# A two-layer gated cross-attention model on one core: in the first expert stage, dispatch three chunks ahead, slot matmuls behind gate and up, other evictions first

## What is computed

```
x = layernorm(x); se = layernorm(slot_embeds) * scale
logits   = einsum('bnd,esd->bnes', x, se)
dispatch = softmax(logits, over the tokens n)
combine  = softmax(logits, over all 1024 slots)
slots    = einsum('bnd,bnes->besd', x, dispatch)
gate     = gelu(slots @ Wg + bg);  up = slots @ Wu + bu
eout     = (gate * up) @ Wd + bd
out      = einsum('bns,bso->bno', combine, eout)
```

## Time and profile before

| | |
|---|---|
| median of 3 runs | 1813.88 us (1812.2 to 1814.11) |
| profiled execution | 1814.76 us |
| its span, first to last instruction | 1813.0 us |
| busy: PE, DVE, ACT, POOL | 1614.1, 1107.4, 951.6, 391.3 us |
| the stage at issue | from 239 to 1141 us of the span |
| gelu, line 883 | 256 times, 687 ns each, with 64 table loads of 1283 ns |

### The profile page before, as it was taken

The page is one execution under the profiler, slowest core; times in us unless marked ns, Lnnn a source line. Parts: engine busy times, 40 slices in busy tenths (PEclk is TensorE's granted clock), DMA queues, the critical chain, the costliest instruction groups (busy, mean ns, idle before and its releaser), DMA issues. The chain is left out here.

```text
span 1813.0 us, 36041 instructions
## 1 busy us (share of the span) xinstructions
PE 1614.1 (89%) x12837; PEld 1316.1 (73%) x12837; DVE 1107.4 (61%) x2407; ACT 951.6 (52%) x1407; POOL 391.3 (22%) x346
## 2 busy tenths in 40 slices
PE   1677589999999999999999999589998878999998
PEld 1566468777777777777777788567777757888887
DVE  6688466656655566655665565446666666555555
ACT  1678356566565666655665666156655644222222
POOL 2234232322222222222222222123222310000000
PEclk9899699999999999999999999799999999999999
DMA  8100000000000000000000000300000020000000
GB/s 221 30 0 1 15 1 2 1 1 2 2 2 3 1 1 2 1 3 1 2 1 2 1 1 2 95 1 1 1 0 0 0 71 1 7 12 6 6 6 12
DMA packets 31171, 23.47 MB, mean 13 GB/s; under 512 B 3161, under 2 KB 28721, under 8 KB 30898
## 3 DMA queue, kind: packets, MB, share of 16 engines
q1 hardware_dynamic: 31026, 21.56, 4.3%
HBM read 19.46 MB, written 2.10 MB: 12 GB/s over the span
## 5 line engine op out<-in xcount | busy, mean ns | idle before, releaser
L762 DVE SCALAR_TENSOR_TENSOR hidden<-psU,b_cols,gelu 128x512 f32<-128x512 f32 x256 | 187.2, 748 | 154.2 <-ACT gelu L883 106.1
L986 PE MATMUL psDown<-w_down,hidden 128*64 128x128 f32 x4096 | 251.9, 276 | 0.8 <-DVE expert_out L768 0.8
L986 PEld LDWEIGHTS psDown<-w_down,hidden 128*64 128x64 f32 x4096 | 220.9, 137 | 18.2 <-issue 8.4
L883 ACT ACTIVATE gelu<-psG,b_cols 128x512 f32<-128x512 f32 x256 | 170.6, 687 | 115.2 <-PE psG L137 112.1
L1635 ACT ACTIVATE silu<-psG 128x512 f32<-128x512 f32 x128 | 76.4, 597 | 213.0 <-PE psG L137 208.1
L717 POOL TENSOR_TENSOR combine_sum<-combine_sum,combineT 128x512 f32<-128x512 f32 x48 | 61.3, 1278 | 493.0 <-ACT combineT L897 493.0
L768 DVE TENSOR_TENSOR expert_out<-psDown,b_down 128x512 f32<-128x512 f32 x128 | 87.9, 687 | 97.6 <-PE psDown L986 93.7
L135 PE MATMUL psG<-slots_hi,w_gate_hi 128*128 128x512 f32 x256 | 110.7, 433 | 26.2 <-DVE slots_lo L863 13.4
L883 ACT ACT_TABLE_LOAD x64 | 82.1, 1283 | 90.1 <-PE psG L137 89.4
L1697 PEld LDWEIGHTS psY<-w_downT,hidden 128*128 128x128 f32 x1024 | 123.9, 191 | 5.8
L1697 PE MATMUL psY<-w_downT,hidden 128*128 128x128 f32 x1024 | 124.3, 275 | 0.0
(11 more groups left out here) (324 smaller groups left out, 3611.6 us busy)
## 6 DMA issues: line engine op xcount, KB each, us to landing
ctx<-in_ctx SPq DMA_DIRECT2D x8, 512.0 KB, 7.1
x<-in_x SPq DMA_DIRECT2D x4, 512.0 KB, 5.6
w_gate_raw<-in_L_ffn_Wg SPq DMA_DIRECT2D x1, 2048.0 KB, 11.9
w_up_raw<-in_L_ffn_Wu SPq DMA_DIRECT2D x1, 2048.0 KB, 17.5
out<-x SPq DMA_DIRECT2D x8, 256.0 KB, 2.3
w_kv<-in_L_xattn_Wkv SPq DMA_DIRECT2D x1, 1024.0 KB
w_down_raw<-in_L_ffn_w_down SPq DMA_DIRECT2D x1, 1024.0 KB, 10.8
kv<-in_L_ffn_slot_embeds SPq DMA_DIRECT2D x1, 512.0 KB, 4.3
```

Source lines behind the costliest of these rows:

```text
L762: dve.scalar_tensor_tensor(hid[e][:, half, :], U[half][:], bcol[:, 1, 4 * ch + 2 * e + half:][:, 0:1], gel[half][:], ALU.add, ALU.mult).th ...
L883: act.activation(gel[half][:], G[half][:], ACT.Gelu, bias=bcol[:, 0, 4 * ch + 2 * e + half:][:, 0:1]).then_inc(s["gelu"], 1)
L986: last = pe.matmul(DN[e * SEQ:(e + 1) * SEQ, j, :], hid[e][:, half, b * SEQ:(b + 1) * SEQ], wd[:, 2 * ch + e, half, :], start=(half == 0 a ...
```

## The change

- Score products, their copies and their maxima all stand at the start of a chunk (`AHEAD`; `FIRST` in the prologue), and alternate between the banks of `psM`.
- Dispatch is made three chunks ahead instead of two. Its transposes are made two chunks ahead, go into `psU1` behind down of half 0, and its copy stands behind `slots_hi` on ScalarE. TensorE waits for that copy ahead of the second gate product.
- The slot matmuls stand directly behind gate and up; down of half 0, combine and transposes follow them.
- `expert_out` of half 0 stands ahead of `mtok`, of `finish` and of `slots_lo`; `slots_lo` stands ahead of the sum of dispatch. `slots_hi` and `slots_lo` signal each half.
- `mb` stands behind down of half 1. x is turned through `psG1`.
- At the end of a chunk ScalarE computes a gelu of one column into `warm`, which nobody reads.

```diff
-EARLY = ((), (), (), (), (2,), (), (5,), (7,))
-LATE = ((), (), (0,), (1,), (3,), (4,), (6,), ())
+AHEAD = ((), (), (), (0, 1), (2, 3), (4,), (5, 6), (7,))
+FIRST = ((), (), (), (0,), (1,), (2,), (3, 4), (5, 6, 7))
...
-    ones = sb("ones_col", [P, 1])
+    ones, warm = sb("ones_col", [P, 1]), sb("warm_col", [P, 1])
...
     G0 = G[0][:].rearrange("p (t s) -> p t s", t=OP)
+    G1 = G[1][:].rearrange("p (t s) -> p t s", t=OP)
+    U1 = U[1][:].rearrange("p (t s) -> p t s", t=OP)
...
-        return M0 if has_core(o) else (M0, M[:, 1, :], G[0][:], G[1][:])[n % 4]
+        if has_core(o):
+            return M[:, 1 if n in (1, 3, 6) else 0, :]
+        return (M[:, 0, :], M[:, 1, :], G[0][:], G[1][:])[n % 4]
...
-                if exists(o, ch, 2):
-                    need(pool, s["eb_inv"], k + 3)
-                    e = eb[ch % 2]
+                if exists(o, ch, 3):
+                    need(pool, s["eb_inv"], k + 4)
+                    e = eb[(ch + 1) % 2]
                     pool.tensor_tensor(e[:], e[:], over(rb[:], SEQ, 2), ALU.mult).then_inc(s["eb_normed"], 1)
...
                 if has_head(o):
-                    for n in EARLY[ch]:
+                    for n in ahead(o, ch):
                         column_max(o, n)
                 if has_core(o):
...
-                if has_head(o):
-                    for n in LATE[ch]:
-                        column_max(o, n)
-                    if ch == 1:
-                        need(dve, s["lnT_hi"], o + 2)
-                        need(dve, s["lb"], 8 * (o + 1))
-                        dve.tensor_tensor(lnT[1][:], G[0][:], lnT[0][:].bitcast(F32), ALU.subtract
-                                          ).then_inc(s["lnT_lo"], 1)
-                    if ch == CH - 1:
-                        need(dve, s["top_t"], o + 2)
-                        need(dve, s["mb"], o + 1)
-                        dve.tensor_reduce(mtok[:], G0, AX.X, ALU.max).then_inc(s["mtok"], 1)
+                if has_core(o):
+                    expert_out(k, 0, ch)
+                if ch == CH - 1 and has_head(o):
+                    need(dve, s["top_t"], o + 2)
+                    need(dve, s["mb"], o + 1)
+                    dve.tensor_reduce(mtok[:], G0, AX.X, ALU.max).then_inc(s["mtok"], 1)
                 if done:
                     finish(o - 1)
-                if has_core(o):
-                    expert_out(k, 0, ch)
+                if exists(o, ch, 1):
+                    i = (ch + 1) % 2
+                    need(dve, s["up"], 4 * k)
+                    for b in range(2):
+                        need(dve, s["sl_hi"], 2 * (k + 1) + b + 1)
+                        hi, lo = (sl[i][n][:].rearrange("p e (t b) n -> p e t b n", b=2)[:, :, :, b, :] for n in (0, 1))
+                        dve.tensor_tensor(lo, M[:, b, :].rearrange("p (t e n) -> p e t n", t=OP, e=2),
+                                          hi.bitcast(F32), ALU.subtract).then_inc(s["sl_lo"], 1)
+                if ch == 1 and has_head(o):
+                    need(dve, s["lnT_hi"], o + 2)
+                    need(dve, s["lb"], 8 * (o + 1))
+                    dve.tensor_tensor(lnT[1][:], G[1][:], lnT[0][:].bitcast(F32), ALU.subtract
+                                      ).then_inc(s["lnT_lo"], 1)
...
-                if exists(o, ch, 1):
-                    i = (ch + 1) % 2
-                    need(dve, s["sl_hi"], k + 2)
-                    need(dve, s["up"], 4 * k)
-                    for b in range(2):
-                        hi, lo = (sl[i][n][:].rearrange("p e (t b) n -> p e t b n", b=2)[:, :, :, b, :] for n in (0, 1))
-                        last = dve.tensor_tensor(
-                            lo, M[:, b, :].rearrange("p (t e n) -> p e t n", t=OP, e=2), hi.bitcast(F32), ALU.subtract)
-                    last.then_inc(s["sl_lo"], 1)
                 if done:
                     keep_fresh(c, dve, o - 1, fresh, bn, s["x_new"], s["bn"])
...
         act.activation(work[:, 0, :], work[:, 0, :], ACT.Sqrt).then_inc(s["inv_b"], 1)
+        act.wait_ge(s["ones_ready"], 1)
...
-                    for n in EARLY[ch]:
+                    for n in ahead(o, ch):
                         keep_raw(o, n)
                 if has_core(o):
                     for e in range(2):
                         for half in range(2):
                             gelu(k, e, ch, half)
-                if has_head(o):
...
-                        keep_raw(o, n)
-                if exists(o, ch, 1):
-                    need(act, s["td"], k + 2)
-                    need(act, s["sl"], k + 1)
-                    act.copy(dn[:], M1).then_inc(s["d_ready"], 1)
...
-                if exists(o, ch, 2):
-                    need(act, s["shifted"], k + 3)
-                    act.activation(eb[ch % 2][:], eb[ch % 2][:], ACT.Exp).then_inc(s["eb_exp"], 1)
+                if exists(o, ch, 3):
+                    need(act, s["shifted"], k + 4)
+                    act.activation(eb[(ch + 1) % 2][:], eb[(ch + 1) % 2][:], ACT.Exp).then_inc(s["eb_exp"], 1)
                 if has_core(o):
...
                 if exists(o, ch, 1):
                     need(act, s["sl"], k + 2)
                     need(act, s["up"], 4 * k)
-                    need(act, s["sl_lo"], k)
+                    need(act, s["sl_lo"], 2 * k)
                     for b in range(2):
                         hi = sl[i][0][:].rearrange("p e (t b) n -> p e t b n", b=2)[:, :, :, b, :]
-                        last = act.copy(hi, M[:, b, :].rearrange("p (t e n) -> p e t n", t=OP, e=2))
-                    last.then_inc(s["sl_hi"], 1)
+                        act.copy(hi, M[:, b, :].rearrange("p (t e n) -> p e t n", t=OP, e=2)).then_inc(s["sl_hi"], 1)
+                if exists(o, ch, 2):
+                    need(act, s["td"], k + 3)
+                    need(act, s["sl"], k + 2)
+                    act.copy(dn[:], U1).then_inc(s["d_ready"], 1)
+                if ch == 1 and has_head(o):
+                    need(act, s["tx"], o + 2)
+                    need(act, s["lb"], 8 * (o + 1))
+                    act.copy(lnT[0][:], G[1][:]).then_inc(s["lnT_hi"], 1)
                 if ch == CH - 1 and has_head(o):
                     need(act, s["mb"], o + 2)
                     need(act, s["ct_sub"], 8 * (o + 1))
                     act.copy(mb[:], G[1][:]).then_inc(s["mb_ready"], 1)
+                if has_core(o) and exists(o, ch, 1):
+                    act.activation(warm[:], ones[:], ACT.Gelu)
         walk(act, body)
...
-            back = 1 if has_core(o) else 4
+            back = (2 if n in (1, 3, 6) else 1) if has_core(o) else 4
             need(pe, s["raw"], j + 1 - back)
...
-            need(pe, s["sl_hi"], k + 1)
-            need(pe, s["sl_lo"], k + 1)
+            need(pe, s["sl_lo"], 2 * (k + 1))
...
-                    for n in EARLY[ch]:
-                        need(pe, s["sl_hi"], k + 1)
-                        need(pe, s["sl_lo"], k + 1)
+                    for n in ahead(o, ch):
+                        need(pe, s["sl_lo"], 2 * (k + 1))
                         scores(o, n)
                 if has_core(o):
                     if ch == 0:
                         need(pe, s["mtok"], o + 1)
                         need(pe, s["mb_ready"], o + 1)
                         need(pe, s["den_inv"], o)
-                    if ch == 2 and has_head(o):
-                        need(pe, s["lnT_hi"], o + 2)
-                        need(pe, s["lnT_lo"], o + 2)
                     for e in range(2):
                         for half in range(2):
+                            if e == 0 and half == 1 and exists(o, ch, 1):
+                                need(pe, s["d_ready"], k + 2)
+                            if e == 0 and half == 1 and ch == 2 and has_head(o):
+                                need(pe, s["lnT_lo"], o + 2)
                             gate_up(k, e, ch, half)
-                if has_head(o):
-                    for n in LATE[ch]:
-                        scores(o, n)
-                if has_core(o) and exists(o, ch, -1):
-                    combine(k - 1, 1, (ch - 1) % CH)
                 if exists(o, ch, 1):
-                    need(pe, s["eb_normed"], k + 2)
-                    need(pe, s["sl_hi"], k + 1)
-                    need(pe, s["sl_lo"], k + 1)
-                    e = eb[i][:].rearrange("p (t b) n -> p t (b n)", b=2)
+                    need(pe, s["d_ready"], k + 2)
+                    if has_head(o):
+                        need(pe, s["raw"], 8 * (o + 1) + len(sum([ahead(o, i) for i in range(ch + 1)], ())))
+                    src = xn[par if ch < CH - 1 else 1 - par]
+                    for b in range(OB):
+                        r = slice((b % 2) * SEQ, (b % 2 + 1) * SEQ)
+                        last = pe.matmul(M[:, b % 2, (b // 2) * P:(b // 2 + 1) * P], src[r, b // 2, :],
+                                         dn[r, b // 2, :], start=True, stop=True)
+                    last.then_inc(s["sl"], 1)
```

(67 more changed lines are left out.)

10 lines of the change are left out of this document (5 added, 5 removed).

## The result

The change makes the kernel **faster: 1768.54 us** (median of 4 runs, 1765.02 to 1769.55) against 1813.07 for the kernel before in the same rounds, a ratio of 0.9748 (95% interval 0.9734 to 0.9763). One launch among the runs further down, of extra_load, took 4013 us where its other three took 1771.6 to 1774.4, and is left out of its figure. The forecast was 1778, with a range of 1764 to 1796. The profiled execution took 1768.40 us, 46.4 less than the one of before; the forecast's sum was 36.1.

A forecast was written before the change was run, and what follows sets the result against it. TensorE's instruction stream was the bound, stalled by a late gelu table load and seams behind slots_lo. 38.4 (loop octets) + 1.1 (straight-line octets) - 1.9 - 1.5 = 36.1 us off 1814.8 gave 1778.7, forecast 1778, range 1764 to 1796.

The forecast's parts named there:

- The sum for a loop octet: Each octet of the loop: 8.5 us of gains less 2.1 given back, 6.4 gained, 38.4 for six.
- 8 x 0.64: Gate and up matmuls in a loop octet: the late table load's 0.64 us stall goes in eight chunks, 5.1 gained.
- the mb wait: Row of column maxima, now behind down of half 1: TensorE waits 0.5 us for its copy, given back per octet.
- slots_lo of chunk 0: Chunk 0: VectorE finishes the old octet first, so slots_lo ends at T+12.3 (T: first gate matmul's start); 0.4 us given back.
- the statistics in chunk 1: Chunk 1: statistics follow the dispatch sum as well, making the first hidden product late; 0.4 us given back with the restart.
- two scores in chunks 4 and 6: Chunks 4 and 6: two scores' maxima stand ahead of the hidden product and make it late; 0.4 us each, 0.8 given back.
- the loop body begins anew three times: I let their first gelu load late: First gelu of each loop body: its table load stays late, 3 x 0.64 = 1.9 us lost (bounds 0 and 2.6).
- which the change leaves: The loop's turns: their cost, included in the 115.6 us per octet, was taken as unchanged by the change.
- The prologue's step: Prologue: a third shift and sum and later maxima on VectorE start the stage at 240.8; 1.5 us lost (bounds 0 and 4).
- A: Each table load holds ScalarE longer than its row, for instance twice, delaying hidden products: 1790 us; chance 0.04.
- B: The table load stays behind the wait on the gate product and only the seams gain: 1807 us; chance 0.06.
- C: VectorE's maxima, stretched beside GpSimd's subtraction, pace the head chunks and make the kernel slower: 1832 us; chance 0.06.

The follow-up runs named there:

- extra_load: The changed kernel with one more table load per chunk, a sqrt of one column ahead of the gelu of one column; 1772.9 us, ratio 0.9775.
- fresh_later: The changed kernel with VectorE's statistics of the finished octet moved from the end of chunk 0 to chunk 1, behind the hidden products; 1760.39 us.
- max_split: The changed kernel with the second maximum of a chunk with two scores moved behind the hidden products; 1766.06 us, ratio 0.9732.
- mb_early: The changed kernel with the transposes of the maxima ahead of dispatch's and the row of maxima ahead of down half 1; 1766.61 us.
- best: The changed kernel with the edits of fresh_later, mb_early and max_split together, still as a loop; 1756.79 us, ratio 0.9688.
- no_warm: The changed kernel without its gelu of one column at the end of a chunk; 1785.84 us, ratio 0.9848.
- slots_late: The changed kernel with the slot matmuls put back behind down of half 0 and combine, dispatch still three chunks ahead; 1779.06 us.
- before_flat: The kernel before with the loop over octets 1 to 6 written out as straight-line code; 1775.26 us, ratio 0.9781.

## Why the prediction was right, and where it was not

**The reading of the bound** was right: stalls within TensorE's busy rows, from the late load and the seam. Both went where the walk said, to a tenth (period 12.14 against 12.2, the 24 gate and up matmuls 5.7 against 5.6, seam 0.54 against 0.53, tiny gelu 0.20 against 0.2, margin 1.13 against 1).

**The sum for a loop octet** came out at 6.3 us (the mean of six; octet 1 alone 6.6) against 6.4, but its parts did not. With the tiny gelu alone an octet gains 4.4 (octet 1, 114.15 to 109.75) against the 5.1 of the step "8 x 0.64": the 5.58 us stream of the kernel before's straight-line octet is not reached, and the load's own part is 0.54. The order adds 2.2 to that (109.75 to 107.59), against 3.4 less 2.1 = 1.3. The two errors cancelled; that the octet's sum came out is luck. Of the four terms given back the sum, 2.1, was right:

- the mb wait: 0.5 forecast, 0.48 measured at the start of octet 1, 0.33 at octets 2, 4 and 6,
- slots_lo of chunk 0: 0.4 forecast, nothing found; it ended at 358.10, T+11.9 instead of T+12.3, and the period is the plain 12.14,
- the statistics in chunk 1: 0.4 forecast, 1.0 measured (fresh_later returned 1.01 there). The step read their length from the earlier trace rows, where x_bn is short; in the new place it ran beside GpSimd's subtraction and took 1.26 us instead of 0.17,
- two scores in chunks 4 and 6: 0.4 each forecast, 0.3 each measured (13.13 against 12.14 and 0.7; max_split returned 0.28).

**The 10 us that were missing** lie outside that octet, in terms mis-sized or left out:

| profiled execution | forecast | measured |
|---|---|---|
| up to the first gate product (239.30 to 238.11) | +1.5 | -1.2 |
| straight-line octets 0 and 7 | -1.1 | -3.7 |
| first gelu of each loop body late | +1.9 | 0 |
| six octets of the loop without the turns | -38.4 | -37.9 |
| the loop's two turns | 0 | -2.8 |
| rest of the kernel | 0 | -0.8 |
| sum | -36.1 | -46.4 |

The step "the loop body begins anew three times: I let their first gelu load late" failed outright: the last tiny gelu of a body had loaded the table already, and a new body needed no load of its own. The step "which the change leaves", of the turns, failed by 2.8: the turns add 2.1 and 2.5 us to the chunk before them instead of 3.2 and 3.3, and a stretch at half clock behind the second adds 1.4 instead of 2.2. The likely reason is that a turn takes in the waits that would stand at its place: in mb_early and best, whose chunk 7 has the wait on the maxima out, the turns add 3.0 to 3.4 again, and the chunk with the turn is no shorter (17.2 to 17.7 against 17.0 and 17.4). No experiment was made for it. In the straight-line octets a seam gave 0.3 us instead of 0.21 (the chunks of octet 7 take 12.14 instead of 12.46), and chunk 0 of octet 7 gave 0.8. The prologue's step expected three shifts and sums ahead of slots_lo to delay the stage; it started 1.2 us earlier. But 1.0 of that lies ahead of the stage's first score product (217.29 against 218.27), where the change does nothing and the fourteen profiles scatter from 216.8 to 219.0. From there to the first gate product pass 20.8 us in the changed kernel and 21.0 in the kernel before: the 1.5 us of the step were 0 or a little less. That the extra work had room beside the waits there is only argued.

**The rivals.** A fell by extra_load. B (the load stays behind the wait) was priced at 1807 and is no_warm, 1785.8: the price took the whole 5.1 per octet back, although in chunks 1, 4 and 6 a late gelu hides behind a late VectorE, and it carried the same missing 10 us. C did not come: in the changed kernel GpSimd's subtraction falls on the statistics, not on the maxima. Slots_late shows it was near: moving one group of matmuls by 2.5 us put it on the maxima.

**The size of the change is a property of the loop.** The prediction noticed that straight-line octets prefetch the load, but drew from it only a smaller gain for two octets. before_flat shows the other reading: writing the loop out gives 39.8 us without the change, nearly as much as its 44.5, and the change then gives 16.4 on top. What the straight-line form gains besides the load are the turns and their half clock (8.8 us in the profiled execution of before), which the change leaves for the most part.

## What to carry to other kernels

In this kernel's loop, whose waits compare a semaphore with a register, the activation-table load stood behind the wait. Look for that in a loop of yours, and pull the load forward with a tiny activation of the next function that waits for nothing, or write the loop out; try the second first, and then look whether the first still helps. Stalls of TensorE shorter than a matmul's drain are seen only in the distances between starts, in a stretch of the same work that runs free. When an order is moved, price each VectorE step by what GpSimd does at its new time, and expect waits in a row to absorb one another.

## What the runs showed of the hardware that was not expected

**VectorE is held until GpSimd is through.** The statistics' x_bn took 166 to 174 ns in all eight octets of the kernel before; in the changed kernel, seven of eight take 1264 ns or more:

```profile
L1725 DVE TENSOR_SCALAR x_bn<-bn_b x8: 171/1264/1269, 360.3 to 1098.5; 128x24 f32 x6, 128x24 f32<-128x24 f32 x2
```

In octet 1 it starts at 360.26 and ends at 361.52, and GpSimd's subtraction, started first, ends at 361.50. The maximum of slots_late ends at 402.08, 0.55 us after the subtraction's end (401.53), which is about the length it has alone, 0.69. By the Trainium skill ("SBUF — State Buffer", SBUF: two separate sides) VectorE and GpSimd hold a shared pair of ports by an exclusive lock for a whole instruction, VectorE where it reads two inputs in SBUF or works in a two-port mode, and the other one stands still; both rows agree. In octet 0 the first x_hat, four instructions beside GpSimd's normalising and its two subtractions, take 3.82 us (three of them 1.08 to 1.32, the last, when GpSimd is through, 0.34):

```profile
238.75 3.82 DVE L814 TENSOR_SCALAR x_hat<-x,x_stats,x_inv 128x128 f32<-128x128 f32 x4
```

**At a turn of the loop TensorE idles for 2.5 to 3.2 us**, in the kernel before and the changed one, with nothing named but issue. The first gate product behind the first turn, in order of time, in the changed kernel and then in the kernel before:

```profile
563.60 0.49 PE L135 MATMUL psG<-slots_hi,w_gate_hi 128*128 128x512 f32 x1 [2.47 <-issue]
```
```profile
579.42 0.50 PE L135 MATMUL psG<-slots_hi,w_gate_hi 128*128 128x512 f32 x1 [3.13 <-issue]
```

Behind the second turn of before, from 810.58 to 816.50, the granted clock is 0.50 (1.2 GHz), where TensorE had just idled; the window around it (columns as in the earlier trace rows):

```profile
810.58:816.50 5.92, 5.92 (x14) 4.66 (x15) 1.15 (x2) 2.66 (x3) 2.03 (x2) 0.50 0.01 4
```

Behind the first turn, after 3.13 us of idle time, it is not. The changed kernel has one such chunk (chunk 0 of octet 5, 13.50 instead of 12.14) and mb_early two, in octets 3 and 5 (13.52); fresh_later has none. With one profile of each, whether that belongs to the kernel or to the launch is not shown.
